# Value weights first, turned and centred on TensorE beside the first recurrence; first two steps written out anew

## The reference, cut to what matters

```
q = silu(x @ Wq);  k = x @ Wk;  v = x @ Wv;  g = x @ Wg
logits = einsum('bhld,hdr->bhlr', v, router_w)      # two routes for each head
scores = softmax(logits); q, k are masked by the chosen route, q scaled by a running count
o = (rotary(q) . rotary(k) * causal) @ v
o = (o - mean(o)) / sqrt(var(o) + eps)              # per head of 64
out = (silu(g) * o) @ Wout
```

## Time and profile before

| what | us |
|---|---|
| median of 3 runs | 1682.52 (1681.97 to 1683.75) |
| the profiled execution, its own time | 1683.49 |
| its span | 1681.7 |
| PE busy | 1550.1 (92%) |
| DVE busy | 1537.5 (91%) |
| ACT busy | 722.3 (43%) |
| POOL busy | 733.5 (44%) |

### The profile page before, as it was taken

How to read it: one execution, slowest core, us unless ns; L and a number is a source line. 1 busy time by engine, 2 the same in 40 slices (tenths; PEclk the granted TensorE clock), 3 DMA queues, 4 the chain that set the end, 5 groups by cost and what they waited for, 6 DMA issues and landing times. The chain is left out here.

```text
span 1681.7 us, 37026 instructions
## 1 busy us (share of the span) xinstructions
PE 1550.1 (92%) x15575; PEld 791.9 (47%) x15575; DVE 1537.5 (91%) x2015; ACT 722.3 (43%) x901; POOL 733.5 (44%) x715
## 2 busy tenths in 40 slices
PE   0425899999999999999999999999999999999997
PEld 0212445555555555555555555555555555555453
DVE  7888999999999999999999999999999999999942
ACT  4825444444434344444334444444343444443320
POOL 1420554444555554444545544445555544445431
PEclk9957899999999999999999999999999999999999
DMA  9500011111111111001111111001111111111101
GB/s 265 214 13 0 26 39 39 36 27 29 35 31 39 39 39 39 27 28 37 27 38 39 39 40 36 27 28 34 31 39 39 39 39 28 28 37 26 26 14 26
DMA packets 23551, 70.74 MB, mean 42 GB/s; under 512 B 2265, under 2 KB 2521, under 8 KB 23385
## 3 DMA queue, kind: packets, MB, share of 16 engines
q1 hardware_dynamic: 23384, 68.37, 14.1%
HBM read 51.59 MB, written 16.78 MB: 41 GB/s over the span
## 5 line engine op out<-in xcount | busy, mean ns | idle before, releaser
L394 PE MATMUL ps_g<-big,h_hi 128*128 128x512 f16 x1536 | 586.6, 382 | 10.7 <-DVE h_lo L1059 5.9
L398 PE MATMUL ps_g<-big,h_lo 128*128 128x512 f16 x1536 | 585.5, 381 | 3.1 <-DVE big L1083 3.1
L395 PE MATMUL ps_g<-big,h_hi 128*128 128x512 f16 x1536 | 586.2, 382 | 0.0
L394 PEld LDWEIGHTS ps_g<-big,h_hi 128*128 128x128 f16 x1536 | 156.4, 102 | 183.3 <-issue 17.0
L398 PEld LDWEIGHTS ps_g<-big,h_lo 128*128 128x128 f16 x1536 | 151.0, 98 | 187.3 <-issue 8.3
L1217 POOL TENSOR_TENSOR small<-small 128x1 f32<-128x1 f32 x64 | 14.3, 223 | 495.4 <-DVE small L845 486.3
L395 PEld LDWEIGHTS ps_g<-big,h_hi 128*128 128x128 f16 x1536 | 150.9, 98 | 164.8 <-issue 3.8
L1236 POOL TENSOR_TENSOR vx<-vx,ek 128x1024 f32<-128x1024 f32 x32 | 75.4, 2357 | 298.2 <-DVE fa L855 287.4
L394 PE MATMUL ps_g<-big 128*128 128x512 f16 x512 | 195.3, 381 | 2.7 <-DVE big L943 2.7
L395 PE MATMUL ps_g<-big 128*128 128x512 f16 x512 | 194.8, 380 | 0.0
L398 PE MATMUL ps_g<-big 128*128 128x512 f16 x512 | 194.7, 380 | 0.0
(11 more groups left out here) (166 smaller groups left out, 2816.5 us busy)
## 6 DMA issues: line engine op xcount, KB each, us to landing
x_ring<-in_x SPq DMA_DIRECT2D x32, 512.0 KB
vx<-in_ctx SPq DMA_DIRECT2D x32, 512.0 KB
out<-x_ring SPq DMA_DIRECT2D x31, 512.0 KB
big<-in_wv SPq DMA_DIRECT2D x2, 2048.0 KB, 21.4
big<-in_wg SPq DMA_DIRECT2D x2, 2048.0 KB, 20.8
big<-in_wout SPq DMA_DIRECT2D x2, 2048.0 KB, 20.1
big<-in_wq SPq DMA_DIRECT2D x1, 2048.0 KB, 14.3
big<-in_wk SPq DMA_DIRECT2D x1, 2048.0 KB, 19.6
```

The source lines that it names most:

```text
L394: nc.tensor.matmul(dst[:, :], hi, hi_of(u)[:, kc * HALF:(kc + 1) * HALF], start=(kc == 0), stop=False)
L395: nc.tensor.matmul(dst[:, :], hi, lo_of(u)[:, kc * HALF:(kc + 1) * HALF], start=False, stop=False)
L398: last = nc.tensor.matmul(dst[:, :], lo, hi_of(u)[:, kc * HALF:(kc + 1) * HALF], start=False, stop=(kc == KC - 1))
```

## The change

The units come in the order v0, v1, q, k, g0, g1, o0, o1. The value weights go through PE: 16 blocks of 128 x 512 are transposed (`turn_block`), copied out by ACT, multiplied by a centring matrix and by the routers (`centre_block`), and split out of PSUM by ACT (`split_centred`) and DVE (`lo_block`). `router_products`, `route_chunk` and `centre` are gone. `tokens_by_time` moves to ACT. Step 0 has its own list on each engine (`first_step`), the recurrence of step 1 begins ahead of it, and the units o0, o1 are split in step 1. Buffers move so that these overlap.

```diff
-UNITS = ("q", "k", "v0", "v1", "g0", "g1", "o0", "o1")
-UQ, UK, UV, UG, UO = 0, 1, 2, 4, 6
+UNITS = ("v0", "v1", "q", "k", "g0", "g1", "o0", "o1")
+UV, UQ, UK, UG, UO = 0, 2, 3, 4, 6
+ROWS = (len(UNITS), 0, 1, 2, 3, len(UNITS) + 1, 4, 5, 6, 7)
...
+        turned = (x_ring[:, 2, 0:HALF], x_ring[:, 2, HALF:C])
+        centring = x_ring[:, 3, 0:P]
+        ones, diag = x_ring[:, 3, P:2 * P], x_ring[:, 3, 2 * P:3 * P]
...
+        ps_v = (ps_g[0], ps_g[1], ps_t[0], ps_t[1])
... SP
+            for dst, src in ((causal_m[:, :], causal), (cos2[:, :], cos_rows), (sin2[:, :], sin_rows),
+                             (cnt_c[:, :], count_rows)):
+                sp.dma_start(dst, src).then_inc(s_tables, 16)
             load_v(0)
             load_unit(0)
+            for n in range(2):
+                sp.dma_start(router_rows[n], router[n:n + 1, :].rearrange("o (m n) -> (o m) n", n=P)).then_inc(s_router, 16)
             load_unit(1)
             sp.wait_ge(s_x, 16)
             load_x(1, 1)
-            for u in range(2, 8):
+            for u in range(2, 5):
                 load_unit(u)
             sp.wait_ge(s_xnp, 2)
             load_v(1)
-            sp.wait_ge(s_wprod, 8)
-            sp.wait_ge(s_wroute, 8)
+            for u in range(5, 8):
+                load_unit(u)
+
+            sp.wait_ge(s_vm, 2 * KC)
... PE
+            def turn_block(m):
+
+                u, kc = UV + m // KC, m % KC
+                pe.wait_ge(s_w[u], 16)
+                after(pe, s_vtc, m - 1)
+                for n in range(4):
+                    last = nc.tensor.transpose(ps_o[m % 2][:, n * P:(n + 1) * P],
+                                               stage_of(u)[:, kc * HALF + n * P:kc * HALF + (n + 1) * P], ident[:, :])
+                last.then_inc(s_vt, 1)
+
+            def centre_block(m):
+
+                u, kc = m // KC, m % KC
+                pe.wait_ge(s_vtc, m + 1)
...
+                after(pe, s_vhi, m - 3)
+                after(pe, s_vlo, m - 3)
...
+                for n in range(4):
+                    block = turned[m % 2][:, n * P:(n + 1) * P]
+                    nc.tensor.matmul(ps_v[m % 4][:, n * P:(n + 1) * P], block, centring, start=True, stop=True)
+                    pair = 4 * u + n
+                    last = nc.tensor.matmul(ps_s[1][:, kc * H + 2 * pair:kc * H + 2 * pair + 2], block,
+                                            routers[:, 2 * pair:2 * pair + 2], start=True, stop=True)
+                last.then_inc(s_vm, 1)
+
+            def first_step():
+                bound_row(4)
+                unit_ready(UQ)
+                project(ps_g[0], h_hi, h_lo, UQ, s_qp, 0)
+                bound_row(5)
+                project(ps_g[0], h_hi, h_lo, UQ, s_qp, 1)
+                unit_ready(UK)
+                project(ps_g[1], h_hi, h_lo, UK, s_kp, 0)
+                bound_row(6)
+                project(ps_g[1], h_hi, h_lo, UK, s_kp, 1)
+                pe.wait_ge(s_rw, 4)
+                route_products(0)
+                route_logits(0)
...
+                project(ps_g[0], h_hi, h_lo, UV, s_vp)
+                sign_sums(0)
...
+                project(ps_g[1], h_hi, h_lo, UV + 1, s_vp)
+                bound_row(7)
...
+                project(ps_g[0], h_hi, h_lo, UG, s_gp)
+                xn_transposes(1, True)
...
+                project(ps_g[1], h_hi, h_lo, UG + 1, s_gp, None, lambda: scores_ready(0))
+                scores(0)
+                bound_row(8)
+                values_ready(0, 0)
+                values(0, 0)
+                bound_row(9)
+                values_ready(0, 1)
+                values(0, 1)
...
+            bound_row(1)
+            for m in range(KC):
+                centre_block(m)
+                turn_block(m + 2)
+            bound_row(2)
...
             xn_transposes(0, False)
+            for m in range(KC, KC + 5):
+                centre_block(m)
+                turn_block(m + 2)
+            bound_row(3)
+            centre_block(KC + 5)
+            turn_block(KC + 7)
+            centre_block(KC + 6)
+            centre_block(KC + 7)
+            pipeline(step, first_step)
... ACT
             exp_k(0, 0)
+            tokens_by_time()
+            routers_by_dim()
             bound_unit(0)
+            copy_turned(0)
+            copy_turned(1)
...
             seed(0)
+            for m in range(4):
+                split_centred(m)
+                copy_turned(m + 2)
+            polynomial(0)
+            for m in (4, 5):
+                split_centred(m)
+                copy_turned(m + 2)
+            split_centred(6)
+            split_centred(7)
             bound_unit(1)
             normed_x(0, 0)
+            copy_turned(8)
+            copy_turned(9)
+            exp_k(1, 1)
+            split_centred(8)
+            split_centred(9)
             silu_h(0)
             split_h(0, 0)
             split_h(0, 1)
+            copy_turned(10)
+            copy_turned(11)
+            split_centred(10)
+            split_centred(11)
+            bound_unit(2)
+            copy_turned(12)
+            copy_turned(13)
+            split_centred(12)
+            split_centred(13)
             split_unit(2)
+            bound_unit(3)
+            copy_turned(14)
+            copy_turned(15)
+            split_centred(14)
+            split_centred(15)
+            seed(1)
             split_unit(3)
+            pipeline(step, first_step)
... ACT, first_step: copy_q, bound_unit(4), copy_k, copy_logits, split_unit(4), polynomial(1), route_prob,
... bound_unit(5), copy_v twice, split_unit(5), normed_x(1), bound_unit(6), bound_unit(7), silu_gate twice,
... exp_k(2), silu_h(1), split_h twice
... ACT, step(1)
+                if i == 1:
+                    split_unit(6)
                 if main:
-                    act.wait_ge(s_qp, i + 1)
+                    copy_q(i)
+                    copy_logits(i)
+                    copy_k(i)
                     route_prob(i)
                 if nxt:
                     seed(n)
+                if i == 1:
+                    split_unit(7)
... DVE
+            def lo_block(m):
+                u, kc = UV + m // KC, m % KC
+                part = slice(kc * HALF, (kc + 1) * HALF)
+                dve.wait_ge(s_vhi, m + 1)
+                V.scalar_tensor_tensor(lo_of(u)[:, part], ps_v[m % 4][:, :], sw[:, u:u + 1], hi_of(u)[:, part],
+                                       ALU.mult, ALU.subtract).then_inc(s_vlo, 1)
... DVE ahead of the loop: lo_block(0) to lo_block(3) between the parts of the ratio, 4 to 7 between output,
... transpose and residual, 8 and 9 after conv_sum(0), h_low(0), denominator_terms(1), 10, 11,
... denominator_scan(1), spread(3), 12, set_scale(3), 13, numerator_turn(1), lo_unit(2), spread(4),
... numerator_terms(1), set_scale(4), 14, 15, route_bound, spread(5), lo_unit(3), split_route_weights(5)
+            def first_step():
+                numerator_pass(1)
+                numerator_add(1)
+                spread(6)
+                ratio_den(1)
+                ratio_num(1)
+                set_scale(6)
+                ratio_correction(1)
+                rotate_q(0)
+                signs(0)
+                lo_unit(4)
+                recurrence_output(1)
+                output_transpose(1)
+                residual(1, 1)
+                spread(7)
+                route_coefficients(0)
+                set_scale(7)
+                turn_heads(s_rk, 0, rot_k, k_sb, s_kt)
+                turn_heads(s_route, 0, route, sgn_t, s_rt)
+                same(0)
+                lo_unit(5)
+                first_norm(2, 2)
+                conv_products(1, 0)
+                conv_products(1, 1)
+                conv_sum(1)
+                spread(8)
+                mask(0)
+                set_scale(8)
+                spread(9)
+                gate_scale(0)
+                set_scale(9)
...
+                h_low(1)
... DVE, step(1): lo_unit(6) after rotate_q(1), lo_unit(7) after numerator_scan(2)
```

More of the change, by code:

```diff
@@ L288, in after, with pipeline @@
                 eng.wait_ge(s, value)
[L290 to L298, removed]
+        def pipeline(step, first):
+            first()
             step(1, 1, True, True, True, True, False)
@@ L419, in step @@
                 if main:
[L420 to L422 removed]
+                    route_products(i)
                     bank_free(i, 1, prev2)
                     project(ps_g[1], h_hi, h_lo, UK, s_kp)
[L425 to L429, removed]
                     route_logits(i)
[L431 removed]
                     after(pe, s_q, i + 1)
@@ L451, in step @@
                     scores(i)
[L452 to L457, removed]
                 if prev:
                     for g in range(2):
+                        if i == 1:
+                            unit_ready(UO + g)
                         if main:
@@ L553, in bound_row @@
                 pe.wait_ge(s_diag, n + 1)
```

(43 more changed lines are left out.)

428 lines of the change are left out of this document (228 added, 200 removed).

## The result

The changed kernel takes 1687.92 us (median of 9 runs, 1683.66 to 1688.92) against 1682.56 before (9 runs). The ratio is 1.0026, with a 95% interval of 1.0015 to 1.0036: slower by about 0.26%, where 1676 was forecast. The forecast's own sign of being wrong, a step 2 that starts after 227, is met too: it starts at 235.13. The profiled execution took 1688.38 us, its span 1686.6.

The account below looks back on a forecast made before the run. PE, busy throughout each later step, keeps its length behind step 2's start; only that start counts: 230.37 - 20.0 (`h_low(1)` earlier) + 12.8 (step 1) = 223.2, a gain of 7.2; forecast 1676 us, 8-in-10 range 1664 to 1689.

Parts of the forecast that it names:

- The forecast's own sign of being wrong: Start of step 2 on PE: forecast near 223; the forecast is wrong if it comes after 227 or before 219.
- the price of a block: Centring blocks on PE with transposes: 3.9 + 0.87 us at 1.2 GHz behind a long wait, 2.4 us each behind that.
- rival A: Opening, slower: PE never leaves 1.2 GHz in blocks 0 to 7, 4.8 us each, 17 us; 1693 to 1700; chance 0.18.
- the term for step 1: Step 1 gets 12.8 us longer: 9.4 of moved DVE work, 3.2 of second effect and slow pace, 0.2 of waits.
- Its other reading: Opening blocks: weight loads of the f32 products don't overlap, about 3.6 us a block, 17 us; part of rival A, chance 0.18.
- The rule of the Trainium skill: Centring blocks over four PSUM banks: PE working through banks in turn idles for moments, often enough to fall to half clock.
- The wait at the sign sums: Step 1: o0's part stands ahead of the signs on DVE, so PE waits about 4 us and is slow after.
- The wait for `gt_lo`: Step 1: PE stands ready when the gate is done, needs 7.4 us, DVE 11.4 to `gt_lo`: a wait of 4.0 us.
- The slow pace behind that wait: Step 1, behind `gt_lo`: 12 matmuls and 8 transposes slow, 2.5 + 0.7 us more before `conv_products(2)` can start.
- Rival B: No change: in step 1 two long PE waits and slow pace after add some 6 us to 12.8; 1682; chance 0.17.
- Rival C: More gained: PE keeps its pace over the 4 us waits in turns with ACT and at `gt_lo`; 11 us, 1665; chance 0.15.
- the walk: Opening through step 1, instruction by instruction: block 7 ends 49.4, block 15 100.3, `h_low(1)` 160.1, 20.0 us earlier than before.

Follow-up runs that it names:

- e5: Changed kernel with each block's four wide products first, then its four narrow ones, nothing left out: 1674.80 us, ratio 0.9951 to the kernel before.
- e6: Changed kernel with an added DVE reduction ahead of each of the four halves of `lo` for o0 and o1 in step 1: 1693.07 us.
- e1: Changed kernel with three of the four narrow router products of each centring block left out: 1658.64 us, ratio 0.9857 to the kernel before.
- four fillers: Changed kernel with PE's and ACT's order changed to cut PE's waits, and an f16 product behind each wide product, four per block: 1670.06 us.
- e12: Changed kernel with two narrow products of 4 columns per block for four of 2, still interleaved: 1664.34 us, ratio 0.9889 to the kernel before.
- e2: Changed kernel with 14 f16 products ahead of the router transpose and 14 ahead of block 0: 1672.96 us, runs in two groups.
- e7: Changed kernel with PE's and ACT's order changed to cut PE's waits, 14 + 14 f16 products ahead, one behind each block: 1676.93 us, two groups.

## Why the prediction was wrong

The step that failed is the price of a block: "I take a block behind a long wait at the slow price and each block behind it at 1.95 + 0.44 = 2.4 us". The fast price was right and somewhat high (2.18 measured in e5). What never came was the fast pace: in the profiled execution all sixteen blocks ran at the slow one, 4.16 with their transposes. The slow price, 3.9 + 0.87 = 4.8 in the prediction, was too high mainly by the narrow products, 0.22 per instruction assumed and 0.14 measured. The 0.50 for the forecast rested on the premise that PE is fast as soon as it has work without a break; no row of before showed that for a stream of this kind, as rival A said.

Point by point. The start, forecast at 28.0 for block 0, came at 26.5 (the first sum ended at 25.7, the unit landed ahead of my 21.9). Block 7 ended near 59 instead of 49.4, `h_low(0)` at 79.2 instead of 67.5, block 15 near 115.5 instead of 100.3, `h_low(1)` at 173.9 instead of 160.1. So `h_low(1)` is 13.8 us late, 10 of them from the first eight blocks: more than the whole miss of 11.9 us (1687.92 - 1676), and the term for step 1 gives 1.85 back. Rival A named this place, its cause (a pace that never rises though PE has work without a break) and its sign. It was priced at 1693 to 1700 with the 4.8, and given 0.18. Its other reading, weight loads that don't overlap, would give 3.6 a block at the fast pace; the slow projection behind the stream speaks against it. The rule of the Trainium skill, "TensorE: Matmul & The Clock Gate", section "A second HAM failure mode: psum-queue depth-cycling", gave the right sign. That going through the banks is not enough to keep the pace down is shown: e5 goes through the same four banks in the same way and gets the fast pace. Whether PE stood idle for moments within a block is not: the profile shows no wait in those 32 us, but short gaps would not show in it.

Step 1 was forecast at 12.8 us more than before; from `h_low(1)` to step 2's first matmul it was 61.24 against 50.29, so 10.95. The wait at the sign sums is there with the forecast 4 us (4.03). The wait for `gt_lo` was 2.77, not 4.0: PE did not stand ready when the gate was done at 208.64 (207.36 + 1.28), it came to its transposes at 210.05.

```profile
207.36 1.28 DVE L1093 TENSOR_TENSOR big<-ps_o,big 128x512 f32<-128x512 f32 x2
...
210.05 1.04 PE L400 MATMUL ps_o<-ident,big 128*128 128x128 f32 x8
```

The slow pace behind that wait lasted for seven matmuls and no transpose, where 12 and 8 were forecast. e6 says that more work of DVE in step 1 is not paid whole. The steps behind are as long as before, as forecast.

Rival B (step 1 gives it back) is refuted by that 10.95. Rival C (PE keeps its pace over waits of 4 us) too: in e5 and e1 the blocks behind such waits start at the slow pace, and in e6 the matmuls behind the wait of 4.51 fell to it after the first two. The rest of the walk, the coupling of the lists, the moved tables, the loads, held in sum: with only the order within a block changed (e5), the forecast is met to 1.2 us. A part of that is luck. In e5 blocks 1 and 2 were slow or partly slow where the forecast had them fast, the walk's 2.5 us for each fast block was 2.18, and `h_low(1)` was late by 1.2 while the blocks ended near 102 instead of 100.3; the errors offset each other.

Not settled: which property of the interleaved stream keeps the pace down. Shown is that a change of order alone lifts it (e5), that fewer narrow products do (e1, e12), and that runs of one kernel can differ by 15 to 20 us (e2, e7). Not tried were narrow products in 16 bits, and a warm-up with no wait between it and block 0 in the interleaved order, which would tell the two readings of e2 apart.

## What to carry to other kernels

A stream in which the profile shows PE busy without a gap is no promise of its fast pace; price a new kind of stream at the slow one until a row shows otherwise, and put products of few columns together rather than between wide ones. When work moves to an engine that was idle, look for the waits that it gets in turn with its suppliers: the order alone was worth 11 us here, the grouping 13, and both with a warm-up made 1658.1 out of 1687.9, 1.4% below the kernel before.

## What the runs showed of the hardware

The granted clock of the profile does not tell the pace: it reads 1.00 for 28 to 60 us of the changed kernel, in which each instruction of a wide f32 product lasted 0.42 us, as at 1.2 GHz, and 0.89 for the same stretch of e5, in which they took 0.28 from 38 us on. The durations of the matmuls tell it. So the clock of 5 to 8 tenths in the earlier trace rows, which rival A took for a sign, need not say at which pace matmuls ran there. And the fall from the fast to the slow pace can come late: PE worked on at the fast pace for 1.7 us behind waits of 1.96 us (e2) and 2.85 us (four fillers), and was slow from there on.
